# Merging paths by a second pair of indices in a two-layer graph kernel, and cutting its products into blocks of 11 in a ring of three

## The reference

```
h = relu(layernorm(x));  x = x + relu(D^-1/2 A D^-1/2 (h W^T + b))      # layer 0
h = relu(layernorm(x))                                                  # layer 1
x1 = h[src] as [E, 16, 32];  x2 = edge_attr as [E, 16, 32]
for each of 64 paths (i1, i2, i3) with coefficient c:
    edge_out[:, i3, :] += c * x1[:, i1, :] * x2[:, i2, :]
x = x + segment_sum(edge_out, dst)
```

## Time and profile before

| what | value |
|---|---|
| median of 3 executions | 1053.53 us (1052.03 to 1053.58) |
| the profiled execution's own time | 1056.4 us |
| its span, first to last instruction | 1054.7 us |
| busy share: DVE, PE, POOL, ACT | 85%, 76%, 48%, 42% |
| mean granted clock of TensorE | 0.859 of full |

### The profile page before, as it was taken

The page is one execution under the profiler, slowest core; times in us unless marked ns, Lnnn a source line. Parts: engine busy times, 40 slices in busy tenths (PEclk is TensorE's granted clock), DMA queues, the critical chain, the costliest instruction groups (busy, mean ns, idle before and its releaser), DMA issues.

```text
span 1054.7 us, 22852 instructions
## 1 busy us (share of the span) xinstructions
PE 797.4 (76%) x5052; PEld 385.5 (37%) x5053; DVE 896.4 (85%) x2196; ACT 444.0 (42%) x1685; POOL 503.4 (48%) x572
## 2 busy tenths in 40 slices
PE   1688887997057787868788786777878687787868
PEld 0334443443023442524344252433425243442517
DVE  4677668844069999999999999999999999999992
ACT  3888887533501532525152242515224251522422
POOL 4222120344643566666454666646466664646500
PEclk7799999999578988888888888888888878888887
DMA  9000000054464667777665677757567775656610
GB/s 168 1 0 0 0 0 1 1 190 146 140 259 151 219 197 272 259 249 262 212 231 182 249 259 258 260 192 247 181 247 259 259 261 203 244 177 243 231 21 11
DMA packets 59518, 183.05 MB, mean 174 GB/s; under 512 B 20116, under 2 KB 20244, under 8 KB 54972
## 3 DMA queue, kind: packets, MB, share of 16 engines
q0 software_dynamic: 27616, 87.97, 26.8%
q1 hardware_dynamic: 22568, 88.88, 22.7%
q10 hardware_dynamic: 9268, 5.55, 1.9%
HBM read 173.71 MB, written 8.66 MB: 173 GB/s over the span
## 4 chain that ended last, share of the span: by engine, by line
PE 25%; DVEq 22%; DVE 21%; issue 18%; ACT 6%; POOL 4%; DMA 2%; ACTq 1%; SPq 1%; POOLq 0%; another core or an unknown queue 0%
DVE q_mem L861 17%; PE psum L1245 14%; DVEq L853 11%; DVEq L856 6%; PE psum L1228 4%; DVEq L861 4%; PE psum L1145 3%; PE psum L1156 2%; ACT S L1075 2%; DVE x_mem L751 2%; ACT hot_mem L1062 1%; DMA x_mem<-in_L_gnn_W 1%; PE psum L1142 1%; POOL x_mem L620 1%; POOL spare L517 1%
## 5 line engine op out<-in xcount | busy, mean ns | idle before, releaser
L861 DVE TENSOR_TENSOR q_mem<-x_mem 128x448 f32 (+2 forms) x1392 | 724.5, 595 | 49.1 <-DMA x_mem<-h_rows,src_now 31.3
L1245 PE MATMUL psum<-q_mem,hot_mem 128*32 128x512 f32 (+1 forms) x2584 | 392.3, 684 | 158.0 <-DVE q_mem L861 118.9
L620 POOL DMA_INDIRECT x_mem<-h_rows,src_now x323 | 395.9, 1226 | 170.9 <-issue 105.1
L1075 ACT ACTIVATE S<-psum,coef 128x32 f32<-128x32 f32 (+1 forms) x800 | 148.1, 335 | 296.4 <-PE psum L1245 231.4
L1245 PEld LDWEIGHTS psum<-q_mem,hot_mem 128*32 128x32 f32 x2584 | 98.1, 128 | 414.9 <-issue 270.0
L1228 PEld LDWEIGHTS psum<-S,place 128*128 128x128 f32 x1600 | 189.0, 196 | 39.2 <-issue 38.9
L1228 PE MATMUL psum<-S,place 128*128 128x32 f32 x1600 | 196.2, 280 | 7.5 <-issue 7.5
L751 DVE TENSOR_SCALAR x_mem<-x_mem,spare 128x320 bf16<-128x320 f16 x323 | 77.4, 296 | 42.1 <-issue 42.1
L1087 ACT ACTIVATE acc<-psum 128x512 f32<-128x512 f32 x12 | 7.2, 597 | 194.8 <-PE psum L1228 194.8
L1156 PE MATMUL psum<-x_mem,hot_mem 128*128 128x320 bf16 x323 | 67.1, 321 | 28.9 <-DVE x_mem L751 18.8
L969 ACT ACTIVATE hot_mem<-x_mem,spare 128x128 bf16<-128x128 f16 x240 | 74.9, 388 | 20.2 <-PE psum L1156 19.7
(11 more groups left out here) (187 smaller groups left out, 454.4 us busy)
## 6 DMA issues: line engine op xcount, KB each, us to landing
x_mem<-in_edge_attr SPq DMA_DIRECT2D x60, 768.0 KB
x_mem<-in_edge_attr SPq DMA_DIRECT2D x35, 1024.0 KB
x_mem<-h_rows,src_now POOLq DMA_INDIRECT x323
out<-acc POOLq DMA_DIRECT2D x12, 256.0 KB, 4.2
x_mem<-in_x SPq DMA_DIRECT2D x1, 2304.0 KB
out<-x_mem ACTq DMA_DIRECT2D x9, 256.0 KB
h_rows<-x_mem ACTq DMA_DIRECT2D x9, 256.0 KB, 2.0
x_mem<-in_L_gnn_W SPq DMA_DIRECT2D x1, 1024.0 KB, 13.6
```

What stands on the lines that cost most here:

```text
L620: pool.indirect_dma_start(x1[:, j * TB + t, :], None, h2_dram[:, :], bass.IndirectOffsetOnAxis(ap=now, axis=0)).then_inc(landed, 16)
L861: return nc.vector.tensor_tensor(q[s % 2][:, 0:tiles, p % PG:p % PG + 1, :], x1_segs[:, first:first + tiles, ds(a, 1), :], x2_segs[:, firs ...
L1075: last = nc.scalar.activation(S[:, p * U:(p + 1) * U], sums, ACT.Copy, scale=coef[:, p:p + 1])
L1245: last = nc.tensor.matmul(ps[s % G][side * M:(side + 1) * M, first * U:end * U], hot[:, j * TB + k, :], q[s % 2][:, k, first:end, :].rearr ...
```

## The change

- **More merging.** A path whose pair (i1, i2) occurs once, and whose (i2, i3) equals that of one earlier such path, is no longer a product of its own. The two x1 segments are added, each with its coefficient, once per node (`combine_segments`, DVE, before a block of `h2` is stored) and stand behind the 16 segments of the row as one of EXTRA = 4 extra segments. The product then reads the extra segment, with coefficient 1. Rows of `h2_dram` and of `x1` grow from 512 to 640 values.
- **The work on the paths moves.** POOL's whole block goes. DVE does the comparisons right at its start, before it waits for the edge indices (`merge_paths`), with six questions to PE (`ask`: DVE hands over, PE multiplies with small matrices, DVE waits for the sums). The three path transfers are now the first of SP's queue. Packing into words (`pack_paths`) stands in DVE's program ahead of `place_items`, in the middle of the aggregation's preparation.
- **Stores one block later.** ACT stores block c - 1 of `h2` behind the activation of block c, when DVE has combined its segments.
- **Blocks and ring.** PG = 11 instead of 16, so six blocks of 11, 11, 11, 11, 11 and 9 positions, and a ring of three slots instead of two. The sixth block (positions 55 to 63) has no slot of its own: its products and sums run ahead of the fifth's, only if more than 55 positions are kept. So a half has five slots. Before slot s DVE waits for slot s - 3. The memsets follow positions 2 and 8 of a block. Mixing of the last three blocks stands behind slots 0, 1 and 2 of the next turn.
- POOL waits for the stores of the first layer's output ahead of the first gather, instead of ahead of each accumulating DMA.

The core of the diff:

```diff
-    G = 4
-    PG = NP // G
+
+    PG = 11
+    G = -(-NP // PG)
+    BLOCKS = [(b * PG, min((b + 1) * PG, NP)) for b in range(G)]
+    RING_Q = 3
+    assert 2 * G % RING_Q == 0
     LATE = 14
     SURE = NP - LATE
 
-    EDGE = 10
-    assert SURE > (G - 1) * PG
+    assert (G - 2) * PG < SURE < (G - 1) * PG
     TURN = 2 * G
 
 
-    MIX_AT, MIX_LAST = {1: [G - 1], 0: [G - 2], G + 1: [0], 2 * G - 1: [1]}, {1: [G - 1], 0: [G - 2], G + 1: [0], G + 2: [1]}
-    MIX_END = [G - 2, G - 1]
+    MIX_AT, MIX_END = {0: [G - 3], 1: [G - 2], 2: [G - 1], G + 1: [0], G + 2: [1], G + 3: [2]}, [G - 3, G - 2, G - 1]
...
+    EXTRA = 4
+    WIDE = D + EXTRA * U
+    PAIR = 512
+    assert 2 * SEGS * SEGS <= PAIR and SEGS + EXTRA <= 2 * SEGS
     FIELDS = [3, 3, 2]
-    WORDS = [-(-NP // 3), -(-NP // 3), PG // 2]
+    WORDS = [-(-NP // 3), -(-NP // 3), LATE // 2]
+    PACKS = [0, WORDS[0], WORDS[0] + WORDS[1], sum(WORDS), sum(WORDS) + WORDS[0]]
...
-    h2_dram = nc.dram_tensor("h2_rows", (N, D), fp32).ap()
+    h2_dram = nc.dram_tensor("h2_rows", (N, WIDE), fp32).ap()
...
-        x1_mem = sb("x1_mem", [P, S4 * T * D], fp32)
-        x2_mem = sb("x2_mem", [P, S4 * T * D], fp32)
-        q_mem = sb("q_mem", [P, 2 * TB * PG * U], fp32)
+        x1_mem = sb("x1_mem", [P, TI * WIDE], fp32)
+        x2_mem = sb("x2_mem", [P, TI * D], fp32)
+        q_mem = sb("q_mem", [P, RING_Q * TB * PG * U], fp32)
...
+            sp.dma_start(path_cols_i, paths).then_inc(paths_in, 16)
+            sp.dma_start(path_vals[:, 3:4], coeffs.rearrange("(n a) -> n a", a=1)).then_inc(paths_in, 16)
+            sp.dma_start(path_rows_i, paths.rearrange("(a n) c -> a (n c)", a=1).broadcast_to([NP, NP * 3])).then_inc(paths_in, 16)
+            sp.wait_ge(pads_set, 3)
...
-            step(nc.gpsimd.partition_all_reduce(repeats, before, P, bass.bass_isa.ReduceOp.add))
-            scalar(repeats, repeats, 1.0, ALU.min)
-            scalar(first, repeats, -1.0, ALU.mult)
-            scalar(first, first, 1.0, ALU.add)
-            rank = count_before(repeats)
...
-            step(nc.gpsimd.partition_all_reduce(laid_sum, laid, P, bass.bass_isa.ReduceOp.add))
-            step(nc.gpsimd.tensor_copy(coef[:, :], laid_sum[:, 4, :]))
...
+                asked = [0]
+
+                def ask(ins):
+                    asked[0] += 1
+                    ins.then_inc(paths_asked, 1)
+                    dve.wait_ge(paths_summed, asked[0])
+                    dve.sem_inc(vector_steps, 1)
+
+                dve.wait_ge(paths_in, 48)
...
+                nc.vector.tensor_scalar(same_pair, pair_row, pair_col, None, ALU.is_equal)
+                link(nc.vector.tensor_scalar(same_goal, goal_row, goal_col, None, ALU.is_equal))
+                nc.vector.tensor_tensor(earlier_goal, same_goal, later, ALU.mult)
+                ask(nc.vector.tensor_tensor(earlier_pair, same_pair, later, ALU.mult))
+
+                nc.vector.tensor_scalar(dropped[:, 0:1], sums[:, 0:1], 1.0, None, ALU.min)
+                ask(nc.vector.tensor_scalar(alone, sums[:, 1:2], 1.0, None, ALU.is_equal))
+
+                nc.vector.tensor_scalar(head, sums[:, 2:3], 0.0, alone, ALU.is_equal, ALU.mult)
+                ask(nc.vector.tensor_scalar(dropped[:, 1:2], sums[:, 2:3], 1.0, alone, ALU.is_equal, ALU.mult))
+
+                link(nc.vector.tensor_scalar(limit, sums[:, 6:7], -1.0, float(LATE), ALU.mult, ALU.add))
...
+                link(nc.vector.scalar_tensor_tensor(first_seg, first_seg, taken[:, 0:1], i1, ALU.mult, ALU.add))
+                link(nc.vector.tensor_tensor(first_seg, first_seg, taken[:, 1:2], ALU.add))
+                for k, val in enumerate((first_seg, i2, i3, path_vals[:, 4:5], new_coef)):
+                    nc.vector.tensor_scalar(by_place[:, k * NP:(k + 1) * NP], across, spread, val, ALU.is_equal, ALU.mult)
+                nc.vector.tensor_copy(n_kept, kept[0:1, :])
+                for k, val in enumerate((head_vals[:, 0:1], head_vals[:, 1:2], taken[:, 2:3], taken[:, 3:4])):
+                    at = 5 * NP + k * EXTRA
+                    last = nc.vector.tensor_scalar(by_place[:, at:at + EXTRA], across[:, 0:EXTRA], taken[:, 1:2], val,
+                                                   ALU.is_equal, ALU.mult)
+                ask(last)
+                nc.vector.tensor_copy(laid, ps[3][:, 0:5 * NP + 4 * EXTRA])
+
+            merge_paths()
 
             dve.wait_ge(idx_in, 16 * 2 * len(by_partition(dst)))
             link(nc.vector.tensor_copy(dst_f, dst_i))
...
+            def pack_paths():
+
+
+                fields = [laid[0:1, k * NP:(k + 1) * NP] for k in range(4)]
...
+                for first, end in BLOCKS[1:]:
+                    link(nc.vector.tensor_scalar(past, fields[3][:, SURE:NP], float(first), float(BANK - PG * U), ALU.is_ge, ALU.mult))
+                    link(nc.vector.tensor_tensor(late, late, past, ALU.add))
...
                 if c == C:
+                    pack_paths()
                     place_items()
...
+            def combine_segments(c):
+
+                s = c % 2
+                dve.wait_ge(h2_ready, c + 1)
+                for n in range(EXTRA):
+                    last = nc.vector.tensor_scalar(scaled_segs[:, n:n + 1, :], h2_segs[:, s, ds(extra_segs[0][n], 1), :],
+                                                   extra_coefs[0][:, n:n + 1], None, ALU.mult)
+                link(last)
+                for n in range(EXTRA):
+                    last = nc.vector.scalar_tensor_tensor(h2_segs[:, s, SEGS + n:SEGS + n + 1, :], h2_segs[:, s, ds(extra_segs[1][n], 1), :],
+                                                          extra_coefs[1][:, n:n + 1], scaled_segs[:, n:n + 1, :], ALU.mult, ALU.add)
+                last.then_inc(extra_ready, 1)
...
                 nc.vector.tensor_scalar(rs2[:, c % 2, 0:1], mv2[:, 1:2], EPS, None, ALU.add).then_inc(var_ready, 1)
+                if c >= 1:
+                    combine_segments(c - 1)
                 dve.wait_ge(root_ready, c + 3)
...
+            def store_rows(c):
+                rows = P if c < C - 1 else LAST
+                act.wait_ge(extra_ready, c + 1)
+                act.dma_start(h2_dram[c * P:c * P + rows, :], h2[0:rows, c % 2, :]).then_inc(h2_stored[c % 2], 16)
...
-                act.wait_ge(h2_ready, c + 1)
-                act.dma_start(h2_dram[c * P:c * P + rows, :], h2[0:rows, c % 2, :]).then_inc(h2_stored[c % 2], 16)
+                if c >= 1:
+                    store_rows(c - 1)
+            store_rows(C - 1)
...
-                return nc.vector.tensor_tensor(q[s % 2][:, 0:tiles, p % PG:p % PG + 1, :], x1_segs[:, first:first + tiles, ds(a, 1), :],
+                return nc.vector.tensor_tensor(q[s % RING_Q][:, 0:tiles, p % PG:p % PG + 1, :], x1_segs[:, first:first + tiles, ds(a, 1), :],
...
-                dve.wait_ge(summed, group(turn, s - 2))
+
+                if block == G - 2:
+                    with dve.If(kept_n > BLOCKS[-1][0]):
+                        dve.wait_ge(summed, group(turn, s + 1 - RING_Q))
+                        dve.sem_inc(vector_steps, 1)
+                        late_products(s + 1, first, tiles, *BLOCKS[-1])
+                dve.wait_ge(summed, group(turn, s - RING_Q))
                 dve.sem_inc(vector_steps, 1)
-                if block == G - 1:
-                    late_products(s, first, tiles, SURE)
-                for p in range(block * PG, min((block + 1) * PG, SURE)):
+                if block == G - 2:
+                    late_products(s, first, tiles, SURE, BLOCKS[block][1])
+                for p in range(BLOCKS[block][0], min(BLOCKS[block][1], SURE)):
                     last = product(s, first, tiles, p)
                     if p % PG in PAUSES:
 
                         cell = (2 * s + PAUSES.index(p % PG)) * (M // 2)
                         nc.vector.memset(pause[:, cell:cell + M // 2], 0.0)
-                last.then_inc(multiplied, 1)
+                last.then_inc(multiplied, 2 if block == G - 2 else 1)
...
+            sums = ps[2][0:NP, :]
+            ones_col, ones_sq = ones[:, 0:1], ones[:, 0:NP]
+            pe.wait_ge(paths_asked, 1)
+            nc.tensor.matmul(sums[:, 0:1], earlier_pair, ones_col, start=True, stop=True)
+            nc.tensor.matmul(sums[:, 1:2], same_pair, ones_col, start=True, stop=True).then_inc(paths_summed, 1)
+            pe.wait_ge(paths_asked, 2)
+            nc.tensor.matmul(sums[:, 2:3], earlier_goal, alone, start=True, stop=True).then_inc(paths_summed, 1)
+            pe.wait_ge(paths_asked, 3)
...
+            pe.wait_ge(paths_asked, 6)
+            nc.tensor.matmul(ps[3][:, 0:5 * NP + 4 * EXTRA], ones, by_place, start=True, stop=True).then_inc(paths_summed, 1)
...
+                def add(s):
+                    n = BLOCKS[s % G][1] - BLOCKS[s % G][0]
                     for t in range(max(b - a for a, b in cut)):
                         for side, (a, b) in enumerate(cut):
                             if t < b - a:
```

(22 more changed lines are left out.)

331 lines of the change are left out of this document (160 added, 171 removed).

## The result

The changed kernel took 1022.67 us (median of 4; 1019.86 to 1027.2), the kernel before 1053.55 beside it: ratio 0.9711, 95% interval 0.9674 to 0.9749. That is faster by 30.9 us, where 46.2 were forecast; the time lies inside the range of 994 to 1032. The profile is the slowest of the four executions (1027.2 us). Further down, where the kernel before is timed on three other chips, its executions more than 1.5% above its fastest are left out. On those chips the changed kernel itself did not run, and kernels made from it were slower than the kernel before; the gain is shown only where the kernel before takes 1053 us.

The account below looks back on a forecast made before the run. The prediction took DVE's products to bound the loop. Its terms (-49.4 + 2.2 - 6 + 1 + 7.5 + 2.5 - 4) summed to -46.2 us, from 1053.5 to 1007.3 us, range 994 to 1032.

Parts of the forecast that it names:

- Products, -49.4: Main loop on DVE: 58 positions become 54, four products fewer in each of 24 halves, 49.4 us less.
- pauses +2.2: Main loop on DVE: nine pauses a half instead of six, 72 more at 0.03 us; 0 to 4.
- Ring, -6: Main loop: three shorter slots remove most of DVE's 7.7 us of waiting for PE; 0 to -7.7.
- Gather, +1: Main loop: wider rows at unchanged 1.50 us pitch arrive about 1 us before DVE; +1 us for late turns, 0 to +8.
- The two gather rivals: Main loop: gather comes late, 1018 to 1050 us (12%); or becomes the bound, 1150 or so (7%).
- Code, 0: Main loop: skipping positions costs nothing by the trace; by the instruction-fetch rule the sum could be 36 us worse.
- code comes late: Rival, main loop: 24 instruction fetches of up to 1.5 us each, up to 1043 us; chance 5%.
- Start, +7.5: Kernel start: merge_paths delays the indices' cast from 13.8 to 23.0 us, of which 7.5 us remain; +3 to +13.
- Before the loop, +2.5: Preparation before the loop: pack_paths and segment combining cost time, POOL's removed path work saves about 6 us; -2 to +7.
- End, -4: After the last product: with blocks of 11 less PE work lies ahead of the last mixing; 0 to -7.
- the narrower one of 994 to 1024: Whole kernel: the main forecast's own range in us, from its terms' bounds, not all at one end; chance 72%.
- the signs that it named: Whole kernel: expected profile readings, such as 1296 products, 216 pauses, 323 gathers; wrong if first product after 308 us.

Follow-up runs that it names:

- e_iota: GpSimd's two iotas moved ahead of its memsets of the kernel's tiles, against the changed kernel; ratio 0.9717 (0.9693 to 0.9741).
- the three remedies: Changed kernel plus an iota behind GpSimd's last all-reduce, ACT clearing all of countsT, last mixing behind PE's fourth slot; 1130.02 us, ratio 1.0586, slow chip.

## Why the prediction was right in sign and 15 us off in size

**Products, -49.4: right.** The means of 614 and 579 ns stand against those of the earlier trace rows, and the loop is 45.4 us shorter with the waits accounted for: -49.4, pauses +2.2, PE +7.2 (14.9 less 7.7), unexplained gaps -6.0, gather +1.3 makes -44.7, within 0.7 of the measured -45.4. The 6.0 us of vanished gaps the prediction had at nothing; they hid nearly half of the 13.2 us that the ring term missed, and that was luck. No run on the first chip takes the merging alone away; the term rests on the count, the means and this sum.

**Ring, -6: the step that failed in the loop.** It came out at +7.2. "I make it about 1 us early" was the error. The changed kernel's PE in the turn from 545 us:

```profile
553.09 4.91 PE L1319 MATMUL psum<-q_mem,hot_mem 128*32 128x352 f32 x28 [3.77 <-ACT S L1126]
557.93 4.90 PE L1300 MATMUL psum<-S,place 128*128 128x32 f32 x22
562.76 4.05 PE L1319 MATMUL psum<-q_mem,hot_mem 128*32 128x352 f32 x28
```

```profile
577.06 2.12 DVE L900 TENSOR_TENSOR q_mem<-x_mem 128x416 f32 x4 [3.03 <-PE psum L1319]
```

PE waits for ACT's 20 late saves and restarts at low clock: 0.50 of full, the level of 1.2 GHz, was granted from 553 to 563 us, so that a slot took 4.91 us and 2.56 later on, and a mixing 4.90 and then 2.64. With three mixings in front the fourth slot is then late for the second half. Of the three waits of 3.0 to 3.8 us two are of this kind; the third, at 726.28 us, stands at the head of a turn, behind a stretch at 0.50 from 707 to 717. Three other executions of the same loop had 7.4 to 8.5 us of waits and none over 1.2: there the clock was back sooner (`e_iota`, restart at 552.19 us: 0.50 from 552 to 557, 0.92 from 557 to 562, and a wait of 0.92). One had 15.8. So the term is between 0 and +8 with the clock, and -6 in none of the five: even at its best the changed ring waits as long as the old one. A sum for PE must be made at the clock at which it restarts, not at its mean.

**Gather, +1: right** (+1.3). Rows of 2560 bytes are issued like those of 2048: 1229 ns against 1226, in the same 27616 packets. The pitch, as the prediction said, goes with DVE's products and not with the bytes: 1.25 us where DVE stands (from 293.37 us), about 1.50 beside products of 416 and 1.61 beside those of 448. The two gather rivals did not come on the first chip, where the gather was late by 1.3 to 4.0 us in all in each of five loops; in the run with the three remedies, on another chip, it was late by 26.7 us.

**Code, 0: right here.** Unexplained gaps fell to 3.9 us, none over 0.6. On the slow chips something that looks like the rival "code comes late" goes with loops 115 to 182 us longer in the four kernels with the changed kernel's ring and merging, on PE and also on DVE, whose first gaps without a releaser, 0.6 to 4.3 us each, lie in the loop's first 20 us. That it is this rival is not shown.

**Start, +7.5: the step that failed most.** It was +18.4, outside its own bound of +13. The work of `merge_paths` was sized 2 us too large: from PE's first answer to the cast it took 11.5 us, with five more questions in it, where 13.6 were reckoned. The cast came 9.2 us later than the forecast 23.0, and the 1.8 us that were to disappear behind it did not. What the prediction left out were two stalls of GpSimd's making: its iota 7.5 us late and its memset in DVE's way for 5.4. They overlap with the wait for PE: without both the cast came at 21.55 us, 10.7 earlier. The trace of before held both: GpSimd's gaps after each all-reduce, and the memset at 5.83 to 11.38, while DVE had nothing to do.

**Before the loop, +2.5: right** (+3.2 at the first gather, +0.3 more to the first product). Of its parts, PE stood 1.6 us behind `pack_paths`, for 2.5, and the last block's line 1057 came 6.5 us later than the start alone explains, for 7. **End, -4: right** within its bounds (-5.7).

By the terms: start +10.9, ring and other waits +6.8, before the loop +1, end -1.7, together the 17 us by which the span misses 1008.5. Two terms, start and ring, lie outside their own bounds. That the time is still inside the range, and by 1.3 us inside the narrower one of 994 to 1024, is in part the luck of the vanished gaps. Of the signs that it named, the products, the 216 pauses and the gather's pitch came; the waits for PE (14.9 us for under 2), the cast (32.23 us for 20 to 27), the first gather (291.88 for 275 to 285) and the first product (313.21, not before 308) did not.

## What to carry to other kernels

When work is removed from an engine, ask what state it left behind for the next execution: the price came at the first iota of the next execution, hundreds of us from the edit. When work is moved, look at what other engines do at its new place, also where they share nothing in the program: a long memset on GpSimd is free beside an idle DVE (5.55 us at 5.83 in the kernel before) and can hold a busy one to its end (5.4 us here, of which 3.1 reached the cast). And a gain that uses up the slack of the full DMA stretches should be timed on more than one chip.

## What was unexpected of the hardware

- GpSimd stalls 5.86 to 11.77 us between an all-reduce and an iota, TENSOR_SCALAR or TENSOR_TENSOR, not between it and a cast, copy or memset, and the state outlives the execution (iota at 10.02 or 2.43 us).
- Twenty GpSimd memsets in a row held a DVE operation 6.43 us, one held it 5.98.
- On three of the chips the kernel before took 1068.6 to 1074.6 us, 1.4 to 2.0% more than on the first, and those made from the changed one were 6 to 15% slower than it. On one of them PE's matmuls came one per 0.74 or 1.44 us while the DMA share was 1.0, against one per 0.13 to 0.15 us on the first chip.
